# A macaron block on one Trainium2 core: attention's outputs kept by head dimension, and the pads written inside attention

## The reference

```python
x = x + 0.5 * ffn(layernorm(x))     # router, top 2 of 8 experts, silu-gated
x = x + attn(layernorm(x))
x = x + 0.5 * ffn(layernorm(x))     # the same weights again

# attn, 16 heads of 16 dimensions
latent = (x @ W_k + x @ W_v) @ W_down_kv
k_rec, v_rec = latent @ W_up_k, latent @ W_up_v
scores = q @ k_rec.T / 16 * exp(-0.01 * |t - t'|)
out = softmax(scores) @ v_rec       # per head, softmax over the 1024 keys
return out @ W_o
```

## Time and profile before

| | |
|---|---|
| median of three runs | 5802.96 us |
| profiled execution, its time | 5809.07 us |
| its span | 5807.0 us |
| TensorE busy | 5300.7 us, 91% |
| VectorE busy | 4623.8 us, 80% |
| ScalarE busy | 3392.9 us, 58% |
| GpSimd busy | 2833.3 us, 49% |
| mean granted TensorE clock | 0.968 of full speed |
| stores of `ob` (256 KB), median from issue to landing | 2.6 us |

### The profile page before, as it was taken

One profiled execution on the slowest core, in us unless ns is written; L12 is line 12 of the kernel. 1 busy time (PEld: TensorE's weight loads), 2 busy tenths in 40 slices (PEclk: granted clock), 3 DMA queues, 4 the chain that ended last, 5 costly groups with the idle time before them and its releaser, 6 DMA issues.

```text
span 5807.0 us, 112537 instructions
## 1 busy us (share of the span) xinstructions
PE 5300.7 (91%) x34816; PEld 3149.6 (54%) x34816; DVE 4623.8 (80%) x14385; ACT 3392.9 (58%) x7117; POOL 2833.3 (49%) x2873
## 2 busy tenths in 40 slices
PE   5559999388999999999999999999999999699997
PEld 5548888234444444444444444444444444588885
DVE  7735555477899899898998989989989998555776
ACT  1125555246676666766767667666676766455553
POOL 6740000244647657566475665765756433300555
PEclk9999999689999999999999999999999999799998
DMA  5533333444555555555455555555554443433887
GB/s 171 174 110 104 105 105 104 132 96 96 134 105 125 116 113 129 111 118 126 104 130 109 117 138 103 129 116 111 130 110 110 110 86 71 145 105 112 244 253 234
DMA packets 538662, 731.83 MB, mean 126 GB/s; under 512 B 80312, under 2 KB 454368, under 8 KB 538080
## 3 DMA queue, kind: packets, MB, share of 16 engines
q1 hardware_dynamic: 488928, 590.35, 41.9%
q0 software_dynamic: 49152, 134.28, 7.7%
HBM read 426.83 MB, written 297.53 MB: 125 GB/s over the span
## 4 chain that ended last, share of the span: by engine, by line
PE 73%; POOL 11%; DVE 9%; issue 4%; DMA 1%; SPq 1%; ACT 1%; POOLq 0%; DVEq 0%; ACTq 0%
PE psum L1344 14%; PE psum L1181 14%; PE psum L397 13%; PE psum L1190 11%; PE psum L415 6%; POOL xs L667 4%; DVE at_mx L1487 3%; PE psum L1194 3%; POOL at_xT L1647 2%; PE psum L386 2%; PE psum L405 2%; PE psum L1239 2%; PE psum L1320 2%; POOL at_Sd L1725 1%; DVE at_Sd L1482 1%
## 5 line engine op out<-in xcount | busy, mean ns | idle before, releaser
L1410 ACT ACTIVATE at_P<-psum 128x512 f32<-128x512 f32 x4096 | 2125.6, 602 | 998.2 <-PE psum L1190 541.9
L1487 DVE TENSOR_REDUCE at_mx<-psum 128x4 f32<-128x512 f32 x3584 | 2216.6, 680 | 183.2 <-PE psum L1181 175.4
L1181 PE MATMUL psum<-at_kst,at_qst 96*128 96x128 bf16 (+3 forms) x7168 | 1596.4, 293 | 73.9 <-DVE at_mx L1487 50.1
L1190 PE MATMUL psum<-at_qst,at_kst 99*128 99x512 bf16 (+3 forms) x5120 | 1461.2, 318 | 40.7 <-ACT at_P L1410 40.6
L1181 PEld LDWEIGHTS psum<-at_kst,at_qst 96*128 96x128 bf16 x7168 | 615.3, 98 | 1350.5 <-DVE at_mx L1487 575.7
L1344 PE MATMUL psum<-at_P,at_V 128*17 128x512 f32 x8192 | 1103.5, 611 | 0.0
L1725 POOL TENSOR_TENSOR at_Sd<-at_Sd,at_m 128x1024 f32<-128x1024 f32 x256 | 484.6, 1899 | 818.9 <-DVE at_m L1496 816.1
L1190 PEld LDWEIGHTS psum<-at_qst,at_kst 99*128 99x128 bf16 x5120 | 490.0, 98 | 177.2 <-ACT at_P L1410 65.2
L1194 PE MATMUL psum<-at_ident,at_Sd 128*128 128x128 f32 x2048 | 563.7, 275 | 0.0
L1482 DVE CUSTOM_DVE_ANT_0 at_Sd<-psum,at_Dm 128x128 f32<-128x128 f32 x2048 | 442.3, 286 | 60.5 <-PE psum L1181 60.1
L708 POOL DMA_INDIRECT m2Y<-ys,m2yi x256 | 244.8, 956 | 494.6 <-DVE m2X L631 418.5
(11 more groups left out here) (271 smaller groups left out, 8141.9 us busy)
## 6 DMA issues: line engine op xcount, KB each, us to landing
parts<-at_pt SPq DMA_DIRECT2D x768, 128.0 KB
at_qst<-parts SPq DMA_DIRECT2D x768, 128.0 KB
at_kst<-parts SPq DMA_DIRECT2D x128, 384.0 KB
m2X<-xs SPq DMA_DIRECT2D x288, 128.0 KB
ys<-m2X SPq DMA_DIRECT2D x288, 128.0 KB, 2.7
m1X<-xs SPq DMA_DIRECT2D x264, 128.0 KB
ys<-m1X SPq DMA_DIRECT2D x264, 128.0 KB, 1.7
at_kst<-parts SPq DMA_DIRECT2D x128, 256.0 KB
```

The costliest lines, as they stand in the source:

```text
L1181: ins = e.matmul(bank[z % 4][:, col - 512 * u:col - 512 * u + ln], self.qst[0:96, s, side, 128 * t:128 * t + 128], self.kst[0:96, s, 1 - s ...
L1190: ins = e.matmul(turns[a % 3][:, q0 - 512 * qh:q0 - 512 * qh + ln], self.kst[0:99, s, side, 128 * kb:128 * kb + 128], self.qst[0:99, s, 1 ...
L1410: e.activation(self.P[:, i % NP, 512 * qh:512 * qh + 512], turns[a % 3], ACT.Exp).then_inc(self.taken.sem, 1)
L1487: e.tensor_reduce(self.mx[:, p % 2, hh, 8 * o + 4 * u:8 * o + 4 * u + 4], of, op=ALU.max, axis=AX.X).then_inc(self.s_read.sem, 1)
```

## The change

1. "norm" and "oturn" go, with `OT`, `rc` and ACT's copies. Outputs stay with dimensions on partitions.
2. In place of "norm", "osend": SP writes the four groups of `Ou` and the denominators of a pair to memory (`oval`, `oden`; 5 DMAs). ACT may reuse `Ou` when those have landed.
3. Once a batch, "oload" for each half of the queries: 8 DMAs that put the denominators of 16 heads on 16 partitions, eight times over (`DN`), and 2 that load the outputs (`OF`, now with a buffer for each half).
4. "oscale" on DVE for each half: one reciprocal of `DN`, 128x512, and two products of `OF` and `DN`, 128x512. "out" waits for that, and W_o is loaded by 16 DMAs in the matching order of rows.
5. In `out_order` the first two "out" of a batch stand three steps later than before, the last two two steps later.
6. The 24 pads move: DVE computes their rows when a part of the routing ends ("padrows"), and SP writes one pad at each of the next steps ("pad"), from `pzero`.
7. At the end of attention "next", three loads of weights and the last "osend" come first; the shares start at the sixth item of `last_order`.
8. At the start, gathers wait for the tables alone, DVE's preset of `kst` moves behind the normalised tokens (item "latent"), and DVE's work on constants comes between the two halves of the first batch.

```diff
     def norm_order(self, p):
-        yield from (None, ("norm", p))
+        yield from (None, ("osend", p))
 
     def out_order(self, b):
         for t2 in range(4):
             yield ("res", b, t2)
+            if t2 == 0:
+                yield from (None, ("oload", b, 0), None, ("oload", b, 1), None, None)
             if t2 % 2 == 0:
-                yield from (None, ("oturn", b, t2 // 2, 0), ("oturn", b, t2 // 2, 1), None)
+                yield from (("oscale", b, t2 // 2), None)
             yield from (None, ("out", b, t2), None, ("store", b, t2), None, None, None, None)
...
+            if kind == "osend":
+                p = at[0]
+                b, h, done = p // 8, 2 * (p % 8), self.o_out[p % 2].sem
+                w.wait_ge(*self.ou_copied.at(p + 1))
+                if b >= 2 and p % 8 == 0:
+                    for ch in range(2):
+                        w.wait_ge(*self.o_in[ch].at(160 * (b - 1)))
+                for hh in (1, 0):
+                    for qh in range(2):
+                        c = 32 * (2 * hh + qh)
+                        e.dma_start(self.oval[b % 2, :, h + hh, 512 * qh:512 * qh + 512], self.Ou[c:c + 16, p % 2, :]).then_inc(done, 16)
+                e.dma_start(self.oden[b % 2, h:h + 2].rearrange("h (q t) -> (h q) t", q=2), self.Ou[16:128:32, p % 2, :]).then_inc(done, 16)
+            if kind == "oload":
+                b, ch = at
+                done, sl = self.o_in[ch].sem, slice(512 * ch, 512 * ch + 512)
+                for i in range(2):
+                    w.wait_ge(*self.o_out[i].at(320 * (b + 1)))
+                if b:
+                    w.wait_ge(*self.s_full("out", b - 1, 2 * ch + 1))
+                for x in range(8):
+                    e.dma_start(self.DN[16 * x:16 * x + 16, ch, :], self.oden[b % 2, :, sl]).then_inc(done, 16)
+                for k in range(2):
+                    e.dma_start(self.OF[:, ch, k, :], self.oval[b % 2, 8 * k:8 * k + 8, :, sl].rearrange("x h t -> (x h) t")).then_inc(done, 16)
...
+            if kind == "oscale":
+                b, ch = at
+                w.wait_ge(*self.o_in[ch].at(160 * (b + 1)))
+                k = own.end(e.reciprocal(self.DN[:, ch], self.DN[:, ch]))
+                w.wait_ge(*k)
+                for k in range(2):
+                    ins = e.tensor_tensor(self.OF[:, ch, k], self.OF[:, ch, k], self.DN[:, ch], ALU.mult)
+                ins.then_inc(self.o_scaled.sem, 1)
...
             if kind == "out":
                 b, t2 = at
-                w.wait_ge(*self.result("oturn", b, t2 // 2, 1))
+                w.wait_ge(*self.wo_in.at(256))
+                w.wait_ge(*self.o_scaled.at(2 * b + t2 // 2 + 1))
...
-                w.wait_ge(*(self.s_full("norm", p - 2) if p >= 2 else self.result("weight", 2)))
+                w.wait_ge(*(self.o_out[p % 2].at(80 * (p // 2)) if p >= 2 else self.result("weight", 2)))
...
             yield from routing()
+            if pads:
+                yield ("pad", pads.pop(0))
...
+        yield from (("pad", r) for r in pads)
+        for _p, items in late:
+            yield from (item for item in items if item)
         yield ("next",)
-        shares = iter([("share_in", 0), ("share_in", 1), ("share_in", 2)] + [
-            item for i in range(24) for item in ((("share_in", i + 3),) if i < 21 else ()) + (("share", i), None)] + [("pads",), None])
+        yield from (("share_in", 0), ("share_in", 1), ("share_in", 2))
+        shares = iter([
+            item for i in range(24) for item in ((("share_in", i + 3),) if i < 21 else ()) + (("share", i), None)])
...
-        for _p, items in late:
-            yield from (item for item in items if item)
-        for item in self.last_order():
+        for n, item in enumerate(self.last_order()):
             yield item
-            yield from share()
+            if n >= 5:
+                yield from share()
...
+            if kind == "latent" and not at[0]:
+                e.memset(self.kst[96:99, :, :, :], 1.0).then_inc(self.ones_set.sem, 1)
...
             if kind == "gather":
-                w.wait_ge(*self.x_in.at(48 * (b + 1)))
+                w.wait_ge(*self.t_in.at(32 * (b + 1)))
```

More of the change, by code:

```diff
@@ L796, in order @@
         gather, units = [(b, self.gather_order(b)) for b in range(1, B)], [(b, self.unit_order(b)) for b in range(1, B)]
-        begun, late, outs, route, after, split = {0}, [], [], [], [], None
+        begun, late, outs, route, after, split, pads = {0}, [], [], [], [], None, []
         def advance(queue):
@@ L1396, in scalar @@
                 self.following.weight_hi(e, w, at[0])
-            if kind == "oturn":
-                b, ch, k = at
-                if ch or b:
-                    w.wait_ge(*self.s_full("out", b if ch else b - 1, 1 if ch else 3))
-                e.activation(self.OF[:, k], of, ACT.Copy).then_inc(self.taken.sem, 1)
             if kind == "step" and at[1]:
```

116 lines of the change are left out of this document (54 added, 62 removed).

## The result

The changed kernel takes 5822.4 us (median of 7 runs, 5817.83 to 5825.63) against 5802.17 us before (7 runs). The ratio is 1.0032, 95% interval 1.0023 to 1.0041: slower by 0.3%, where 5798 was forecast. The profiled execution took 5823.48 us, 14.4 more than the one before; two later runs of the same kernel beside the kernel before gave 1.0035 and 1.0033.

The account below looks back on a forecast made before the run. TensorE was taken to bound some 147 us of each 235.5 us batch, the chain jumping between engines in the other 89. Terms: -82 - 15 + 92 - 6 + 6 = -5 us, so 5804 profiled, 5798 median; range 5742 to 5840.

Parts of the forecast that it names:

- burst: VectorE's reciprocal and two products of one half in one piece, 4.74 us, twice a batch: 30 at 3.06, 92 us.
- the sign that the prediction named for itself: Attention's repetition, forecast at 235.1 us: the forecast is wrong if it moves by over 0.8 us either way.
- What goes: Transposes of norms and "oturn" leave TensorE, 82 us; half of the score weights' waits on VectorE goes, 15 us.
- What comes: Work added: on VectorE the burst, 92 us; on SyncE 60 more DMAs a batch, taken at 0.
- the bound stretch: 2550 to 2697 us of a batch: the chain is on TensorE, busy 146.3 of 146.6 us.
- The first half: Burst before a projection and the diagonal blocks: TensorE stands from 4.42 to 6.83, 2.4 us.
- The second half: Burst right behind the diagonal blocks: TensorE has work to 2.3, its next bank is read at 5.35, 3.0 us.
- my 0.36: Microseconds added per burst for its products' wait for GpSimd, a choice between 0 and twice 1.8.
- waits on the norm: Score weights waited 29.9 us for VectorE's norm line to give its bank back; half taken as gain, 15 us.
- Rival (c): SyncE's queue becomes the new wait, rows of maxima come late: +60, 5858 us; chance 0.06.
- Start and end: Start: gather no longer waits for tokens, preset moves into idle time, -6 us. End: block loads later, +6 taken.
- (b): VectorE becomes the bound, at the second half's burst and products waiting for GpSimd: 5836 to 5859 us; chance 0.22.

Follow-up runs that it names:

- e12_shift: Kernel before with only its four `out` of each batch moved to their steps in the changed kernel, two or three later: ratio 0.9856.
- e10: Changed kernel with reciprocal and products cut to 4 of 512 columns and, from the second batch on, no DMAs of the outputs: ratio 0.9664.
- e1b: Changed kernel with reciprocal and products of each half cut to 4 of 512 columns, all DMAs kept, first kind of chip: ratio 0.9709.
- c0_after: The changed kernel itself, unedited, run again beside the kernel before as a yardstick: 5822.8 us, ratio 1.0035.
- e14b: Kernel before with `out` shifted as in e12_shift plus the change's start, preset and pads, no new way of outputs: ratio 0.9849.
- e3: Changed kernel with denominators inverted once as 128x128, stored, then spread over partitions, `out` four steps later: ratio 1.0308, second kind of chip.
- e11_norm_cut: Kernel before with VectorE's part of each norm cut to 4 elements a partition, transposes and waits kept: ratio 0.9997.
- e4: Changed kernel with the two products of each half on GpSimd instead of VectorE, except in the last batch: ratio 0.9865.
- e4b: Repeat of e4, against the kernel before: ratio 0.9851.
- e1: The same edit of the changed kernel as e1b, run on the second kind of chip: ratio 0.9929, 232.8 us a batch.

## Why the prediction was wrong

The stretch from the first to the last products with the values, by kernels that differ in one thing each, on the first kind of chip:

| step | kernels | us | forecast |
|---|---|---|---|
| `out` and router later | e12_shift - before | -85 | 0, not named |
| new way without burst and DMAs | e10 - e12 | -104 | -82 - 15 |
| DMAs | e1b - e10 | +19 | 0 |
| burst | c0_after - e1b | +178 | +92 |
| sum | | +8 | -5 |

(9.6 in the profile shown above; c0_after's is 1.9 shorter. e10 holds start and pads as well, which in e14b are 5 us of the stretch.) The steps add up in this order alone: the shift was taken in the kernel before, and no run has the changed kernel with `out` in the old steps, so what it is worth beside the burst is not shown. The time from the last products on adds 11.6, the start takes 3.9 off, and the rest of the second feed-forward is 2.6 us shorter; with the 9.6 that is the 14.7 us between the two spans. The forecast missed by 24 us in all, and behind it stand two errors of some 85 us each that nearly cancel. That they cancel is luck: by the sign that the prediction named for itself, a batch that moves by over 0.8 us, it would have passed (235.8 us in the median after, 235.5 before). The burst is the term that made a gain a loss; the shift, left out, hid most of it.

**The step that failed first: "What goes" and "What comes" count what each item costs and nowhere where it now stands.** `out` and the router's items behind it move by two or three steps. That was in the diff and in the order, and I priced it at nothing by leaving it out. It is worth -85 us. The earlier trace rows had the sign of it: TensorE idle 7.2 us of the 235, all but 0.3 in the 89 us outside the bound stretch. In e12_shift 3.3 us of the idle time are gone a batch, and the mean granted clock of a batch is 1.00 instead of 0.986, by an estimate (1.4% of 235 us) worth as much again.

**The second: the size of the burst.** The reciprocal was right, 3.35 us against 3.38. The Trainium skill gives the reciprocal a repeat count of 8 (VectorE: DVE Perf Modes, First, the fixed hardware budget); read as eight cycles a column, that is an estimate of 4.4, and the measurement decides against that reading. The first half was right too: TensorE stands 2.47 us, 2.4 forecast. The second half was 3.0 plus 0.36 for GpSimd and is 6.27. Of it 2.15 is the wait for GpSimd, as the fourteenth batch shows, where the same products took 1.29 us instead of 3.44 and TensorE stood 4.13. It struck the second half in 13 of 15 batches and the first in none. So my 0.36, "between 0 and twice 1.8", was the wrong kind of number: a mean over a thing that either always or never happens in a given place of the order. The place was to be looked up: whether GpSimd works there (6.14 of 6.30 us), and on what. In the same 13 batches GpSimd was at work beside the first half too, but with gathers, and there the products took 1.29 us; beside the second half stood its product of two tensors. The Trainium skill says that a two-input product of VectorE and an operation of GpSimd that reads SBUF exclude each other (SBUF — State Buffer, Who interferes with whom). With 3.44 us, and with 7.61 us for 1.38 in e3, the trace agrees.

The last 1.1 us is the order of two items. TensorE's row behind the second burst of the fourteenth batch and of the fifteenth, which has no projection left; in both VectorE's products took 1.29 us:

```profile
4617.24 1.22 PE L1289 MATMUL psum<-at_lat,at_wuk 64*128 64x512 f32 x1 [4.13 <-DVE at_mx L1521]
4834.88 0.39 PE L1228 MATMUL psum<-at_kst,at_qst 96*128 96x256 bf16 x2 [3.15 <-DVE at_mx L1521]
```

In the fifteenth TensorE does the products with the values (0.98 us) ahead of the stand, as the forecast of 3.0 assumed, and stands 3.15. In the fourteenth, as in the others, a projection stands in the order ahead of them and waits for a bank, so they can't cover anything.

And what no term had: behind the stand of 6.27 the granted clock is 0.50 for some 5 us. Steps 23 and 24 together are 8.7 us shorter without the burst, the stand being 6.3. The burst is 12.6 us a batch (sum of the steps' medians), the two stands 8.7 of it.

**The transposes.** -0.44 us in the steps of the norms and -0.9 in those of "oturn" between e12_shift and e10: as forecast. 15 x 5.26 is 79 of the 104. The other 25 stand where I had 15 us for waits on the norm. e11_norm_cut shows that in the old order 0.5 us of VectorE's 0.8 a pair were worth nothing, and in the trace of the kernel before no product of TensorE waited for that line: the 29.9 us of the earlier trace rows are waits of weight loads, beside products still running. So the reason that I gave was wrong and the number not far off by luck; what the 25 are is not shown.

**SyncE.** Rival (c) was there in small, 19 us of its 60, and 1.15 us at one place of a batch: the stack behind a send that the late projection held back, rather than the rows of the maxima.

**Start and end.** The start is -3.9 for -6. The normalised tokens were 6.2 us earlier, but "covered, just" was wrong: 2.62 us of issue, the preset's 10.30 and the clearing of `pzero` fill more than 13 us where 10.59 had been idle, and VectorE took the first projection at 1089.8 instead of 1093.4, 3.6 us earlier and not 6.2. At the end every one of my times, moved by the 5.7 us that attention ended later, was early by a little: `out` starts at 4974.09 (4973.4), the last split is done at 5015.1 (5012.7), the block loads start at 5037.03 (5033.2). The second reciprocal stands on the chain between two splits. Taken away one after the other, the burst is 9 us of the end (e1b) and the DMAs 11 (e10).

**The rivals.** (b) comes nearest, "the burst of the second half, behind the diagonal blocks, where VectorE is already behind, and the products that wait for GpSimd": the place and the mechanism are those found, and the waits, 2.47 x 15 + 6.27 x 13 + 4.13 + 3.15 = 126 us, are past the 110 that I had set for it. Its 5836 to 5859 missed for the same reason as the forecast, the gain of the shift.

**Versions that beat both.** Without any part of the new way, the plan's shift with start and pads (e14b) is 0.9849; the new way with its products on GpSimd (e4, e4b) 0.9865 and 0.9851. The two can't be told apart, and either beats the changed kernel by 1.7 to 1.9%, on the first kind of chip. The new way is then worth nothing over the old with the same steps; without its burst it would be worth 1.4% more (e1b).

## What to carry to other kernels

When an edit of a written order adds or removes an item, everything behind it moves: take the moved items as a term of its own, and test it alone, with empty items in the kernel before. What such a shift gives can be 85 us in one set of runs and 9 in another, so compare only within a set. Price a burst by the place where it stands: on what GpSimd works in those microseconds, what unit TensorE needs next, and the slower clock behind a long stand. An operation moved to another queue brings its wait with it, and what is behind it there waits too.

## What the runs showed of the hardware that I had not expected

- Two products of 128x512 with both inputs in SBUF take 1.29 us alone or beside GpSimd's gathers (13 batches), 3.44 beside its product of two tensors (13 batches), and 7.61 beside four of its operations in a row. The reciprocal, with one input, was 3341 to 3352 ns in all 32.
- Behind a stand of 6.27 us the granted clock was 0.50 for 4 us and 0.67 for two more; behind 2.42 us of standing 0.57 over 4 us; behind 2.74 us in e4 it stayed 1.00. The length of the last stand alone doesn't say which.
- The reciprocal costs 6.2 to 6.3 ns for each further column: 0.17 us on 4 columns, 0.95 on 128, 3.35 on 512.
- One kernel (e1) differs by 4% between two sets of runs, on two chips, in the length of a batch, most of it in five steps of 64, with exponentials of 0.60 us on both.
